# Moving the sums of the residual path's weights to GpSimd in group 0, and loading the last projection's low weights whole

## The reference, cut to what matters

```python
x = (x - mean) / (1e-06 + std) / math.sqrt(P)
x = _conv2d(x, conv1_w, conv1_b)                       # 3 -> 64 channels, 3x3
residual = x
x = _gelu(_group_norm(x, gn1_g, gn1_b))
x = _conv2d(x, rconv1_w, rconv1_b)                     # 64 -> 64, 3x3
x = _gelu(_group_norm(x, gn2_g, gn2_b))
x = _conv2d(x, rconv2_w, rconv2_b)                     # 64 -> 64, 3x3
x = residual + x
x = _conv2d(x, proj_w, proj_b, stride=P, pad=0)        # 64x16x16 -> 192
```

## Time and profile before

| | us |
|---|---|
| median of 3 runs | 1599.48 (1593.47 to 1605.23) |
| profiled execution, device time | 1601.61 |
| profiled execution, span of the trace | 1599.8 |
| TensorE busy | 1455.8 (91%) |
| VectorE busy | 1136.8 (71%) |
| ScalarE busy | 841.1 (53%) |
| GpSimd busy | 582.9 (36%) |
| mean granted TensorE clock | 0.957 of full speed |

### The profile page before, as it was taken

How to read it: one execution, slowest core, us unless ns; L and a number is a source line. 1 busy time by engine, 2 the same in 40 slices (tenths; PEclk the granted TensorE clock), 3 DMA queues, 4 the chain that set the end, 5 groups by cost and what they waited for, 6 DMA issues and landing times. The chain is left out here.

```text
span 1599.8 us, 42535 instructions
## 1 busy us (share of the span) xinstructions
PE 1455.8 (91%) x13394; PEld 1029.1 (64%) x13394; DVE 1136.8 (71%) x4230; ACT 841.1 (53%) x2118; POOL 582.9 (36%) x1111
## 2 busy tenths in 40 slices
PE   6969996888999999999999998999999487899999
PEld 2424442333688588768867885886788486565747
DVE  7724335999888988888888888888888622383710
ACT  1212223777767776666776776677776302323442
POOL 2000003555544544545555554545444201242500
PEclk9989997999999999999999999999999797967999
DMA  6463325433555455445545554554555758000000
GB/s 179 130 196 89 101 88 214 105 99 97 148 147 144 123 147 136 132 125 146 143 124 146 143 134 119 147 145 119 149 147 142 208 152 183 1 1 1 1 2 14
DMA packets 117216, 190.62 MB, mean 119 GB/s; under 512 B 18251, under 2 KB 86282, under 8 KB 116940
## 3 DMA queue, kind: packets, MB, share of 16 engines
q1 hardware_dynamic: 117068, 188.60, 43.1%
HBM read 103.34 MB, written 21.30 MB: 78 GB/s over the span
## 5 line engine op out<-in xcount | busy, mean ns | idle before, releaser
L363 POOL TENSOR_TENSOR sb_tmp<-sb_mst,sb_half_neg 128x8 f32<-128x8 f32 x200 | 354.6, 1773 | 681.1 <-DVE sb_mst L789 681.1
L501 PE MATMUL rc<-sb_acts,sb_rwd 128*64 128x512 f16 x1764 | 562.8, 392 | 16.3 <-DMA sb_acts<-sb_hst 15.8
L502 PE MATMUL rc<-sb_acts,sb_rwd 128*64 128x512 f16 x1764 | 563.7, 392 | 0.0
L417 ACT ACTIVATE sb_f32q<-c,sb_gsh,sb_gsc 128x128 f32<-128x128 f32 x792 | 298.8, 459 | 282.6 <-POOL sb_gsh L373 282.6
L501 PE MATMUL rc<-sb_acts,sb_rwl 128*64 128x512 f16 x1176 | 364.2, 392 | 5.5 <-issue 5.5
L502 PE MATMUL rc<-sb_acts,sb_rwl 128*64 128x512 f16 x1176 | 363.7, 391 | 0.0
L556 PE MATMUL pj<-sb_wall,sb_arena 128*64 128x384 f16 x1792 | 310.0, 336 | 21.9 <-DMA sb_wall<-w_lo 15.3
L425 ACT ACTIVATE sb_g2f<-rc,sb_gsh,sb_gsc 128x128 f32<-128x128 f32 x784 | 298.2, 483 | 4.5 <-POOL sb_gsh L373 4.5
L560 PEld LDWEIGHTS pj<-sb_wall,sb_arena 128*64 128x64 f16 x1792 | 219.2, 222 | 63.4
L560 PE MATMUL pj<-sb_wall,sb_arena 128*64 128x192 f16 x1792 | 240.6, 246 | 0.0
L556 PEld LDWEIGHTS pj<-sb_wall,sb_arena 128*64 128x64 f16 x1792 | 215.4, 218 | 39.0 <-DMA sb_wall<-w_lo 16.8
(11 more groups left out here) (162 smaller groups left out, 1786.0 us busy)
## 6 DMA issues: line engine op xcount, KB each, us to landing
sb_acts<-sb_hst SPq DMA_DIRECT2D x792, 78.8 KB, 2.6
sb_wall<-w_lo SPq DMA_DIRECT2D x56, 528.0 KB, 3.8
sb_im<-x_planes SPq DMA_DIRECT2D x202, 136.5 KB
sb_wall<-w_lo SPq DMA_DIRECT2D x28, 480.0 KB, 3.7
sb_f32q<-in_proj SPq DMA_DIRECT2D x12, 576.0 KB, 4.0
sb_arena<-in_proj SPq DMA_DIRECT2D x12, 576.0 KB, 4.5
w_lo<-sb_arena SPq DMA_DIRECT2D x1, 6144.0 KB, 17.3
scratch_fold<-sb_wall SPq DMA_DIRECT2D x48, 123.8 KB
```

The source lines that it names most:

```text
L363: ch.did(gp.tensor_tensor(t1, var, half_neg[:, :], ALU.pow))
L417: ins = nc.scalar.activation(g1f[:, q * Q + m, :], c1[q][:, m * HALF:(m + 1) * HALF], ACT.Gelu, bias=gsh[q][:, m:m + 1], scale=gsc[q][:, m ...
L501: nc.tensor.matmul(out[0:CH, :], w_odd, x_odd, start=(n == 0), stop=(n == 14))
L502: yield nc.tensor.matmul(out[CH:128, :], w_even, x_even, start=(n == 0), stop=(n == 14))
```

## The change

The sums that make wr move from VectorE, behind the loop, to GpSimd, inside group 0. There GpSimd's program is a generator of 63 steps (one memset, 54 additions over both halves of the outputs at once, 8 additions for the bias), of which three, in every third slot four, are called behind `norm` in the slots k = 7 to 25. T is loaded colour by colour (four DMAs each) into b1 by SP behind the units 3, 4 and 8 of group 0, and wr is stored behind unit 13, the last. ScalarE and VectorE wait before group 1 for this store (`s_wr`) instead of `s_wst`.

Behind the loop the low weights no longer come in chunks into the two small buffers: SP waits for the projection of group 5 (`s_pj`), and loads all of them in six pieces (`LAST`) into b1, each with a semaphore of its own. So that one access pattern reaches high and low weights, `wall` and both halves of the arena are one tensor now, `wall_arena`. GpSimd's group 0 is written out instead of looped.

```diff
+LAST = (0, 8, 24, 50, 76, 102, 128)
...
+        TOT = WALL + 4 * G * HALF
+        wa = sb("wall_arena", [128, TOT], F16)
+        wall = wa[:, 0:WALL]
+        b1, b0 = wa[:, WALL:WALL + 2 * G * HALF], wa[:, WALL + 2 * G * HALF:TOT]
...
-        arena = sb("arena", [128, 2, 2 * G * HALF], F16)
-        g2 = arena[:, :, :].rearrange("p b (h g n) -> p b h g n", h=2, g=G)
+        g2 = [b[:, :].rearrange("p (h g n) -> p h g n", h=2, g=G) for b in (b0, b1)]
...
-        wr = [f32q[0:E // 2, 0:WR + 1], g2f[0:E // 2, :, :].rearrange("p a b -> p (a b)")[:, 0:WR + 1]]
...
+        b1c = b1f[:, 0:4 * COL].rearrange("p (i e t n) -> p i e t n", i=2, e=2, n=DENSE)
+        tbias = b1f[:, 4 * COL:4 * COL + 2 * DENSE].rearrange("p (e n) -> p e n", e=2)
+        wr = b1f[:, 4 * COL + 2 * DENSE:4 * COL + 2 * DENSE + 2 * (WR + 1)].rearrange("p (e n) -> p e n", e=2)
...
+            def load_colour(c):
+                for e in range(2):
+                    for half in range(2):
+                        n = 27 * half + 9 * c
+                        sp.dma_start(b1c[:, c % 2, e, 9 * half:9 * half + 9, :].rearrange("p t n -> p (t n)"),
+                                     ts[e * (E // 2):(e + 1) * (E // 2), n:n + 9, :].rearrange("e t n -> e (t n)")
+                                     ).then_inc(s_tc[c % 2], 16)
+
+            def residual_io(at):
+                if at == 3:
+                    sp.wait_ge(s_wst, 16)
+                    sp.wait_ge(s_ts[0], 32 * (FU // 2))
+                    sp.wait_ge(s_ts[1], 32 * (FU // 2))
+                    load_colour(0)
+                    for e in range(2):
+                        sp.dma_start(tbias[:, e, :], ts[e * (E // 2):(e + 1) * (E // 2), TR - 1, :]).then_inc(s_tb, 16)
+                if at == 4:
+                    load_colour(1)
+                if at == 8:
+                    sp.wait_ge(s_tcd, 1)
+                    load_colour(2)
+                if at == 13:
+                    sp.wait_ge(s_tcd, C + 1)
+                    for e in range(2):
+                        sp.dma_start(wrd[e * (E // 2):(e + 1) * (E // 2), :], wr[:, e, :]).then_inc(s_wr, 16)
...
             def group(g, b, first):
-                if not first:
-                    sp.wait_ge(s_wst, 16)
                 for j in range(GU // 2):
                     for p in range(2):
                         u = g * GU + 2 * j + p
@@ -297,6 +323,8 @@
                         double(2 * u + 3, 1 - p, 1)
                         if not first and 2 * j + p < NCH:
                             load_chunk(g, 2 * j + p)
+                        if first:
+                            residual_io(2 * j + p)
...
-            sp.wait_ge(s_ts[0], 32 * (FU // 2))
-            sp.wait_ge(s_ts[1], 32 * (FU // 2))
-            load_chunk(GROUPS, 0)
-            load_chunk(GROUPS, 1)
-            for e in range(2):
-                sp.dma_start(tbias[:, e, :], ts[e * (E // 2):(e + 1) * (E // 2), TR - 1, :]).then_inc(s_tb, 16)
-            for m in range(4):
-                load_colour(m)
-            load_chunk(GROUPS, 2)
-            load_colour(4)
-            load_chunk(GROUPS, 3)
-            sp.wait_ge(s_tcd, 1)
-            load_colour(5)
-            for c in range(4, NCH):
-                load_chunk(GROUPS, c)
-            sp.wait_ge(s_tcd, C)
-            for e in range(2):
-                sp.dma_start(wrd[e * (E // 2):(e + 1) * (E // 2), :], wr[e]).then_inc(s_wr, 16)
+            sp.wait_ge(s_pj, GROUPS)
+            for i in range(len(LAST) - 1):
+                sp.dma_start(b1[:, LAST[i] * E:LAST[i + 1] * E],
+                             wlod.ap()[:, LAST[i] * E:LAST[i + 1] * E]).then_inc(s_wl[i], 16)
...
-            over_groups(pool, lambda g, b, first: over_units(pool, g, pair, first))
+
+            def residual():
+
+                pool.wait_ge(s_wst, 16)
+                gp.memset(wr[:, :, :], 0.0).then_inc(s_wz, 1)
+                n = 1
+                yield
+                for c in range(C):
+                    pool.wait_ge(s_tc[c % 2], 64 * (c // 2 + 1))
+                    o = wr[:, :, c * P * P:(c + 1) * P * P].rearrange("p e (r k x) -> p e r k x", k=2, x=P)
+                    T = b1c[:, c % 2].rearrange("p e t (s x) -> p e t s x", x=P)
+                    pool.wait_ge(s_wz, n)
+                    for ky in range(3):
+                        for kx in range(3):
+                            for py in range(2):
+
+                                d = py - ky + 1
+                                half, off = (0, (d + 1) // 2) if d % 2 else (1, d // 2)
+                                lo, hi = max(0, kx - 1), min(P, P + kx - 1)
+                                dst = o[:, :, :, py, lo:hi]
+                                pool.wait_ge(s_wz, n - 1)
+                                gp.tensor_tensor(dst, dst, T[:, :, 9 * half + 3 * ky + kx, off:off + 8, lo - kx + 1:hi - kx + 1],
+                                                 ALU.add).then_inc(s_wz, 1)
+                                n += 1
+                                yield
+                    pool.wait_ge(s_wz, n)
+                    pool.sem_inc(s_tcd, 1)
+                pool.wait_ge(s_tb, 32)
+                for dst, x, y in ((0, 72, 72), (0, 36, 36), (0, 18, 18), (0, 9, 9), (0, 4, 4), (0, 2, 2), (0, 1, 1)):
+                    gp.tensor_tensor(tbias[:, :, 0:x], tbias[:, :, 0:x], tbias[:, :, y:y + x], ALU.add).then_inc(s_wz, 1)
+                    n += 1
+                    pool.wait_ge(s_wz, n)
+                    yield
+                gp.tensor_tensor(wr[:, :, WR:WR + 1], tbias[:, :, 0:1], tbias[:, :, 8:9], ALU.add).then_inc(s_wz, 1)
+                n += 1
+                pool.wait_ge(s_wz, n)
+                pool.sem_inc(s_tcd, 1)
+                yield
...
+            work = residual()
+            for k in range(2 * GU):
+                norm(k + 3, 1 - k % 2)
+                for _ in range(3 + (k % 3 == 0) if 7 <= k <= 25 else 0):
+                    next(work, None)
+            with pool.Fori(0, (GROUPS - 1) // 2) as i:
+                for g in (2 * i + 1, 2 * i + 2):
+                    over_units(pool, g, pair, False)
...
-            act.wait_ge(s_wst, 16)
+            act.wait_ge(s_wr, 32)
...
+            def project(b, n0, n1, whole=False):
 
                 for n in range(n0, n1):
                     c = max(k for k in range(NCH) if CHS[k] <= n)
-                    to_low = (HALF + (c % 2) * WCH + n - CHS[c] - n) * E
-                    both = bass.AP(tensor=wall, offset=n * E, ap=[[WALL, 128], [to_low, 2], [1, E]])
+                    to_low = WALL if whole else (HALF + (c % 2) * WCH + n - CHS[c] - n) * E
...
-            for c in range(NCH):
-                chunk_waits(GROUPS, c)
-                last = run(project(0, CHS[c], CHS[c] + CHN[c]))
-                last.then_inc(s_pj if c == NCH - 1 else s_pc, 1)
+            pe.wait_ge(s_sp2, 2 * GU * GROUPS + 2)
+            pe.wait_ge(s_pjr, GROUPS)
+            for i in range(len(LAST) - 1):
+                pe.wait_ge(s_wl[i], 16)
+                last = run(project(0, LAST[i], LAST[i + 1], True))
+            last.then_inc(s_pj, 1)
...
-            dve.wait_ge(s_wst, 16)
+            dve.wait_ge(s_wr, 32)
...
-            dve.wait_ge(s_pj, GROUPS)
-            dve.wait_ge(s_sp1, K + 2)
-            dve.wait_ge(s_sp2, K + 2)
-            for e in range(2):
-                v.memset(wr[e], 0.0).then_inc(s_wz, 1)
-            n = 2
...
-                            for e in range(2):
-                                T = tc_[(2 * c + e) % NTC].rearrange("p t (s x) -> p t s x", x=P)
-                                o = wr[e][:, c * P * P:(c + 1) * P * P].rearrange("p (r k x) -> p r k x", k=2, x=P)
-                                o = o[:, :, py, lo:hi]
-                                dve.wait_ge(s_wz, n - 1)
-                                v.tensor_tensor(o, o, T[:, 9 * half + 3 * ky + kx, off:off + 8, lo - kx + 1:hi - kx + 1],
-                                                ALU.add).then_inc(s_wz, 1)
-                                n += 1
```

42 lines of the change are left out of this document (8 added, 34 removed).

## The result

The changed kernel takes 1634.34 us (median of 5, 1618.45 to 1635.82) against 1599.48; the ratio is 1.0186 [1.0144, 1.0227]. On another chip it was 1630.83 against 1605.12, 1.0156 [1.0107, 1.0205]. The forecast was 1616, range 1602 to 1632: the sign was right, the time 18 us too low and 2 us over the range's end.

What follows compares the result with a forecast made beforehand. It took VectorE to bound group 0, and the last projection, waiting for low weights queued behind T, the stretch after the loop. Terms -19.3 + 9 + 3 + 14 + 7 + 3 = +16.7 gave a 1616 us median, range 1602 to 1632.

Steps and rivals of the forecast that it cites:

- Point 1: Last projection behind the loop: no more waits for low weights, tokens start earlier, -19.3 us (bounds -21 to -10).
- Point 2: Slot 7 of group 0: GpSimd waits for T's first colour, making the power late, +9 us (bounds 6 to 13).
- T lands in time: Rival for group 0: colours arrive before GpSimd needs them, additions hidden; -10 us, 1589, chance 0.07.
- Point 3: Slot 18 of group 0: GpSimd waits for T's third colour, a smaller stall, +3 us (bounds 1 and 7).
- point 6: Group 0: SP's copies queued behind T land 1 to 2 us late and TensorE's clock drops, +3 us (0 to 7).
- Point 4: Group 0: GpSimd's additions each block VectorE's two-SBUF-input instructions by 0.30 us, +14 us (bounds 2 to 27).
- The rule that I set against the row: Trainium skill: VectorE instructions with two SBUF inputs and GpSimd instructions reading SBUF exclude each other, whole waits; 27 us.
- Point 5: End of group 0: ScalarE and VectorE wait for the store of wr, +7 us (5.5 to 9).
- hidden additions: Rival for group 0: GpSimd's additions fall between VectorE's two-input instructions; +5 us, 1605, chance 0.20.
- Full exclusion: Rival for group 0: each addition blocks VectorE for its whole length, 27 us; sum +30, 1629, chance 0.16.
- The one on the other side: The not-slower rival: T lands in time in group 0, additions hidden; -10 us, 1589, chance 0.07.

Runs made afterwards that it cites:

- e1: Changed kernel without T's loads and all 62 additions, wr zeroed and stored behind unit 9; low weights still loaded whole: ratio 0.991 to the kernel before.
- e8: Kernel before, SP's queue behind the loop reordered, each chunk of low weights ahead of the next half colour of T: ratio 1.0013 to the kernel before.
- e7: Kernel before with low weights loaded whole behind the loop, T in twelve quarter-colours between them, sums still on VectorE: ratio 0.9909 to the kernel before.
- e9: e7 with two of the six pieces of low weights queued later among the quarter-colours: ratio 0.9926 to the kernel before.
- e6: Changed kernel without the 54 additions; T's loads, bias sums and store of wr stay in place: ratio 1.0071 to the kernel before.
- e3: Changed kernel with T's three colours loaded behind units 1, 2 and 7 instead of 3, 4 and 8: ratio 1.0142 to the kernel before.
- e5: Changed kernel with T's twelve loads spread over units 0 to 3, 6 and 7, wr stored behind unit 12: ratio 1.0059 to the kernel before.
- e4: e2 with one tensor_scalar of VectorE's moments replaced by a scalar_tensor_tensor with a constant tile: ratio 1.0103 to the kernel before.
- e10: e5 without the 54 additions; spread loads and store behind unit 12 stay: ratio 0.9956 to the kernel before.
- e2: Changed kernel with each of the 54 additions replaced by a GpSimd memset of about the same length: ratio 1.0129 to the kernel before.
- e11: e5 with GpSimd's additions waiting in slots 6 to 24 until VectorE has finished the next half's moments: ratio 1.0081 to the kernel before.

## Why the prediction was right in sign and low in size

- **Point 1, the last projection (-19.3):** -19.4. Right, mechanism and size; e1 shows it alone (-18.4 at the tokens, with 1.2 us later start). By e8, e7 and e9 order alone brings 2.7 us of it, room for all low weights with T still in the queue 11 to 12, and the rest comes with T gone.
- **Point 2, the first colour (+9):** +9.4 (14.09 less 4.67). Right in size, half right in mechanism. e6 and e3 show that the copies behind the colour would have cost as much, had GpSimd not waited. The rival "T lands in time" rested on this point, and was wrong in saying that a start not tied to the copies of half 9 would save the stall: e3 is that start, and saved nothing; what saved the stall was spreading the loads (e5).
- **Point 3, the third colour (+3), and point 6, late copies and clock (+3):** together 9.2 instead of 6. The slot of the third colour took 10.48 us, 4.6 more than one with additions only; the copies behind the second colour cost 3.8 and 0.8 in two slots. The failed step is the sentence that the copies land when the colour has drained, 11 to 12 us after its first load, and so come 1 to 2 us late. Three of each four did; the fourth landed 16.0 and 16.3 us after it, and TensorE, which asked 12.6 and 10.0 us after it, waited 3.46 and 6.33 us. The clock that this point also feared did fall: 0.54 granted in the 6.3 us behind the first of these waits, with TensorE busy throughout; its share of the 9.2 is not separated.
- **Point 4, the additions beside VectorE (+14):** mis-sized. Twelve undisturbed addition slots cost 1.26 us more each, 15.2, and with the same in three more slots that other waits lengthened about 19; the difference of the changed kernel and e6 is 16.2. I had one block of 0.30 us for each addition. By the runs it is three two-input instructions in a slot with 0.25 to 0.34 us more each (505, 511 and 426 ns against 175), 0.92 us in the mean, and length on top where four steps fall into one slot (e4). The list in the forecast lacked one of these three (L775, now L828), which starts just as `norm` ends, and had L808, L787 and L789 instead, which the additions hardly touch (692 to 713 ns, 167 to 214, 167 to 167). My additions were too short as well: 0.58 us estimated, 708 and 766 ns in the mean for the two sizes. The rule that I set against the row was right in kind, a wait to the end of the running addition (e5's rows: 0.65 to 0.69 us for instructions of 0.175). As a price, 27, it was too high, since VectorE, as I read it, often arrives when part of the addition is done.
- **Point 5, the end of group 0 (+7):** +7.6 over two slots (10.45 and 6.31 us against 4.42 and 4.78). Right.
- Sum in group 0: 44.2 measured, 36 forecast; at the tokens +24.4 instead of +16.7. The first profiled execution took 1618.45 us, what the sum gave, but only because its tail ran 7.8 us shorter at a higher clock. In the second profile the tail was 5.8 us longer than in the profile of before; of the 15.7 us by which that execution (1633.96) lies above the sum, some 9 are group 0's and 5.8 the tail's. I had left the tail out as unchanged; its work is, its clock isn't, and it moved these profiles by up to 14.6 us. Eight of nine executions of the changed kernel took 1630 us or more. Whether the long tail comes oftener with this kernel stays open: 29 executions of the kernel before ranged from 1590.94 to 1610.44 beside e8 to e10, which fits tails of both lengths too.
- **The rivals:** hidden additions are refuted by e5's rows and by e4. Full exclusion gave 1629 for its price of point 4, nearer to the median than my 1616, but by an excess that stood for costs elsewhere; its own mechanism is shown. The one on the other side had its chance (0.07) from a wrong condition.

Net: the change wins 19.4 us behind the loop and pays 44.2 in group 0. By e1, e6 and the changed kernel the bill in group 0 is 2 us for what e1 keeps (the memset of wr and its store), 26 for T's loads in blocks and the late store, and 16 for the additions.

## What to carry to other kernels

Loads of 2 MB in the queue of small copies that the pipeline needs stalled it at both places tried; spread in pieces they cost 7.6 us instead of some 20. So ask what stands behind a load, and just ahead of it, before asking who waits for it. (Whether another engine's queue would spare the copies, no run tests.) An idle engine beside a saturated one is only free if their instructions do not hold each other up: look at which instructions of the saturated engine fall into the idle time, and check in the rows of a control that it holds up none of them, as e2's memsets did and e4's did not. And undo a change in halves: here one half won 18 us and the other lost 43.

## What the runs showed of the hardware that was not expected

- A memset on GpSimd (write only, 691 ns) lengthens VectorE's tensor_scalar of 128x16 float32 from 167 to 967 ns and leaves the two-input instructions that do not stand behind it at 175 to 188; additions (two reads) lengthen the two-input ones to 426 to 511 ns. The tensor_scalar can be held past the memset that is running: beside three memsets in a row (349.92 to 351.89 in e2) one takes 1.22 us from 350.05 on, to about the end of the second.
- The exclusion works both ways: in e11 the same additions take 827 and 905 ns in the mean instead of 736 and 768 in e5.
- Four copies of 79 KB issued one after the other behind a colour of 2 MB do not land together: three land 6.4 to 7.2 us after their issue, the fourth 10.5 to 10.7 (12.4 and 12.9 where the next colour follows at once, in e6 and e3).
- The tail takes 272 us at a granted clock of 0.90 and 286 us at 0.86, in executions of one kernel on the same inputs; TensorE's busy time for its 1434 matmuls is 237 and 249 us.
